# Lead-in of an attention and expert kernel: order of the first loads, row writes and stack loads, and the place of three batches' statistics

## The reference

```
x = x + L0_xattn(layernorm(x), ctx, ctx)   # 16 heads of 16, time bias -0.1 |tq - tk|
x = x + L0_ffn(layernorm(x))               # product-key experts + dense
x = x + L1_xattn(layernorm(x), ctx, ctx)   # relu projections
x = x + L1_ffn(x)                          # 8 experts, top 2
```

## Time and profile before

| what | value |
|---|---|
| time, median of 3 runs | 1219.52 us (1215.89 to 1220.21) |
| the profiled execution: time, span | 1213.62 us, 1211.8 us |
| TensorE, VectorE, ScalarE, GpSimd busy share | 87%, 65%, 53%, 39% |
| chain that ended last, by engine | PE 55%, DVE 24%, ACT 8%, issue 6%, POOL 3%, DMA 3% |
| mean granted clock | 0.928 |

### The profile page before, as it was taken

The page is one execution under the profiler, slowest core; times in us unless marked ns, Lnnn a source line. Parts: engine busy times, 40 slices in busy tenths (PEclk is TensorE's granted clock), DMA queues, the critical chain, the costliest instruction groups (busy, mean ns, idle before and its releaser), DMA issues.

```text
span 1211.8 us, 16920 instructions
## 1 busy us (share of the span) xinstructions
PE 1055.4 (87%) x5478; PEld 658.8 (54%) x5478; DVE 788.4 (65%) x1986; ACT 638.7 (53%) x848; POOL 474.4 (39%) x494
## 2 busy tenths in 40 slices
PE   9499899989776999999999778999999888799991
PEld 5134343434355787787777554433334334588881
DVE  3667677786489777877787334777777955244443
ACT  2146565566528667667677422565545661355550
POOL 1347777686413243343443321212323334222220
PEclk9579999999879999999999986999998998899996
DMA  7946778666999300000002330455453328222226
GB/s 186 249 148 192 228 198 264 174 206 224 255 238 233 78 1 1 1 1 1 1 1 64 103 78 1 148 165 146 117 167 93 102 63 325 66 74 71 72 62 209
DMA packets 75595, 151.71 MB, mean 125 GB/s; under 512 B 8234, under 2 KB 45356, under 8 KB 73974
## 3 DMA queue, kind: packets, MB, share of 16 engines
q1 hardware_dynamic: 62518, 99.46, 31.9%
q0 software_dynamic: 10544, 47.23, 11.2%
q10 hardware_dynamic: 2448, 3.94, 1.2%
HBM read 73.88 MB, written 76.25 MB: 124 GB/s over the span
## 4 chain that ended last, share of the span: by engine, by line
PE 55%; DVE 24%; ACT 8%; issue 6%; POOL 3%; DMA 3%; SPq 1%; ACTq 0%; DVEq 0%; POOLq 0%
PE ps L1296 14%; DVE negmax L1589 9%; PE ps L1194 7%; PE ps L1161 6%; PE ps L1140 4%; PE ps L1175 4%; PE ps L1149 4%; PE ps L1398 3%; PE ps L1375 3%; PE ps L1361 2%; PE ps L1203 1%; PE ps L1516 1%; DVE moe_w L1885 1%; DVE hl L1594 1%; DVE on L1609 1%
## 5 line engine op out<-in xcount | busy, mean ns | idle before, releaser
L1589 DVE TENSOR_REDUCE negmax<-ps 128x1 f32<-128x512 f32 x512 | 320.9, 682 | 68.9 <-PE ps L1161 67.2
L905 ACT ACTIVATE pt<-ps 128x1024 f32<-128x1024 f32 x256 | 256.4, 1026 | 129.9 <-PE ps L1175 129.1
L1161 PE MATMUL ps<-sk,sq 56*128 56x512 f32 x512 | 166.5, 460 | 48.0 <-DVE negmax L1589 24.7
L1194 PE MATMUL ps<-pt,v_aug 128*32 128x512 f32 x1024 | 142.6, 620 | 1.2 <-POOL pt L670 0.8
L1161 PEld LDWEIGHTS ps<-sk,sq 56*128 56x128 f32 x512 | 75.7, 200 | 105.3 <-DVE negmax L1589 76.3
L1175 PE MATMUL ps<-sq,sk 57*128 57x512 f32 x512 | 127.1, 489 | 2.5 <-DVE negmax L1589 1.4
L670 POOL TENSOR_TENSOR pt<-pt,near 128x256 f32<-128x256 f32 x128 | 92.3, 728 | 76.0 <-ACT pt L905 75.7
L1175 PEld LDWEIGHTS ps<-sq,sk 57*128 57x128 f32 x512 | 50.1, 190 | 101.2 <-issue 72.4
L835 POOL DMA_INDIRECT expert_out<-yo,dest x39 | 38.2, 980 | 116.2 <-ACT yo L1080 104.5
L751 POOL TENSOR_TENSOR w_first<-w_first,moe_w 128x1024 f32<-128x1024 f32 x16 | 38.1, 2379 | 105.7 <-DVE pt L1877 105.0
L1361 PE MATMUL ps<-sel,hl 128*128 128x512 f32 x256 | 71.7, 412 | 5.6 <-DVE pt L1877 5.6
(11 more groups left out here) (284 smaller groups left out, 2008.2 us busy)
## 6 DMA issues: line engine op xcount, KB each, us to landing
expert_rows<-zero SPq DMA_DIRECT2D x3, 5586.0 KB, 58.0
expert_weights_split<-wst POOLq DMA_DIRECT2D x8, 2048.0 KB, 9.4
qk_rows<-hl SPq DMA_DIRECT2D x30, 512.0 KB
sq<-qk_rows SPq DMA_DIRECT2D x60, 192.0 KB, 4.6
sk<-qk_rows SPq DMA_DIRECT2D x60, 192.0 KB, 5.1
moe_w<-in_w POOLq DMA_DIRECT2D x16, 512.0 KB, 7.1
wexp<-expert_weights_split POOLq DMA_DIRECT2D x16, 512.0 KB, 4.6
wexp<-expert_weights_split SPq DMA_DIRECT2D x4, 2048.0 KB, 17.1
```

Of the source, the lines that this page charges most:

```text
L905: act.activation(pt[:, 4 * (U % 2) + 2 * half:4 * (U % 2) + 2 * half + 2, :], ps[:, 2 + 2 * half:4 + 2 * half, :], ACT.Exp, scale=(BIAS, S ...
L1161: pe.matmul(ps[:, jbank(job), :], sq[r, pair, t * P:(t + 1) * P], sk[r, pair, :], start=True, stop=True).then_inc(s_job, 1)
L1194: ins = pe.matmul(ps[32 * j:32 * j + 32, OBANK, :], v_aug[:, b % 2, c, HG * g + j, :], pt[:, 4 * (U % 2) + j, :], start=(c == 0), stop=(c ...
L1589: dve.tensor_reduce(negmax[:, n % 2, col:col + 1], src, AX, ALU.max, negate=True).then_inc(s_jd, 1)
```

## The change

It rewrites the order of the lead-in on all engines, and moves the statistics of batches 1 to 3.

- VectorE makes `rowc` first, as soon as its source is in, then batch 0's statistics and norm, then scales the Q weights. Its `prologue()` is gone. The statistics of batches 1, 2 and 3 (`batch_stats`) stand at the ends of steps -4, -3 and -2, the reciprocal at the end of step -1.
- SP issues the constant rows and the rows of K directly behind the constants, then `w_ret` and `keys`, then all eight stacks of K; only when group 0 of both stacks is in does it issue x of batches 1 to 3, the next context and the selector.
- ScalarE issues the rows of Q ahead of emptying V, then all eight stacks of Q. It copies the folded weights out of PSUM, takes the square root of batches 1 to 3 and then `near`'s exponential.
- GpSimd issues six of the weight loads, scales the gate weights, subtracts the low parts of `wret` at steps 4 and 8, and adds `bo` at later steps.
- TensorE runs `keep_busy(4)` behind the folded weights; the gate products stand at the end of step -4. In the first attention K of a batch now stands before its norm's transposes (steps -1 and 0 for batch 1, 11 and 12 for batch 2).

```diff
-STACKS = (None, 10, 12, 12)
-NEXT_CTX = (-LEAD, -9)
+PREPARE_1 = {-17: ("k", 0), -16: ("k", 1), -15: ("xt", 0), -14: ("xt", 1), -13: ("q", 0), -12: ("q", 1), -11: ("v", 0), -10: ("v", 1)}
+PREPARE_2 = {-21: ("k", 0), -20: ("k", 1), -17: ("xt", 0), -16: ("xt", 1), -15: ("q", 0), -14: ("q", 1), -12: ("v", 0), -11: ("v", 1)}
+STACKS = ((None, 10, 11, 11), (None, 10, 12, 12))
+NEXT_CTX = ((2, -9), (-LEAD, -9))
...
+            sp.dma_start(st_rows, a["c_rows"]).then_inc(s_rows_in, 16)
...
             sp.wait_ge(s_rowc, 1)
+            for dst in (sk, sq):
+                for s in range(2):
+                    const_rows(sp, 0, s, dst)
+            for s in range(2):
+                write_rows(0, 0, "k", s)
+            for dst, src in ((st_wq, a["w_ret"].rearrange("(a n) d -> n a d", n=RD)), (st_keys, a["keys"].rearrange("n h p k -> n (h p k)"))):
+                sp.dma_start(dst, src).then_inc(s_wr, 16)
+            sp.wait_ge(s_dk, 64)
+            for g in range(NG):
+                for s in range(2):
+                    stack(0, 0, g, s, sk)
+            sp.wait_ge(s_ld[0], 64)
+            sp.dma_start(x_tok[:, 1], tokens(a["x"][1])).then_inc(s_x[1], 16)
+            load_ctx(0, 1)
+            sp.dma_start(st_sel, a["c_sel"]).then_inc(s_selin, 16)
+            for b in range(2, B):
+                sp.dma_start(x_tok[:, b], tokens(a["x"][b])).then_inc(s_x[b], 16)
...
+            gate_columns()
             norm(0, 1)
+            bias_out()
...
+                    for k in range(KC):
+                        act.wait_ge(s_wret_ps, k + 1)
+                        act.copy(wret[:, 0, k, :], ps[:, 2 + k, :]).then_inc(s_wret, 1)
+                        act.copy(wret_full[:, k, :], ps[:, 2 + k, :]).then_inc(s_wret, 1)
+                    sqrt(1, sd[:, 1:B, :], mv[:, 1:B, :, 1])
+                    act.wait_ge(s_ci, 16 * NCI)
                     act.activation(near[:], st_dist, ACT.Exp, scale=-BIAS).then_inc(s_nr, 1)
...
                 if L == 0:
                     prologue()
+                    keep_busy(4)
+                pe.wait_ge(s_rowin[L], 16 * NROW)
...
+                    if L == 0 and U == -4:
+                        gate_prologue()
...
+                    if L == 0 and U in (-4, -3, -2):
+                        batch_stats(U + 5)
+                        if U == -2:
+                            dve.sem_inc(s_lnv, 1)
+                    if L == 0 and U == -1:
+                        dve.wait_ge(s_lnd, 2)
+                        dve.reciprocal(rstd[:, 1:B, :], sd[:, 1:B, :]).then_inc(s_rstd, 1)
...
+            def batch_stats(b):
+                dve.wait_ge(s_x[b], 16)
+                stats(TT * b, x_tok[:, b], range(TT))
+                moments(TT * b, mv[:, b])
...
+            dve.wait_ge(s_rows_in, 16)
+            dve.tensor_copy(rowc[:], st_rows).then_inc(s_rowc, 1)
             dve.wait_ge(s_x[0], 16)
```

More of the change, by code:

```diff
@@ L611, in _, with gate_columns, wret_low, bias_out @@
                 pool.memset(dst, value).then_inc(s_ms, 1)
+            for dst, src in (
+                (bo_bc[:], a["bo"].rearrange("(a n) -> a n", a=1).broadcast_to([P, D])), (bvc[:], a["bv"]),
+                (gw[:, :, 0:ME], kcut(a["gate"])), (gcol[:, 0:KC], a["gamma"]),
+                (gcol[:, KC:2 * KC], a["beta"]), (wo[:], kcut(a["wo0"])),
+            ):
+                pool.dma_start(dst, src).then_inc(s_w, 16)
+            own = Own(pool, s_pown)
+            def gate_columns():
+                pool.wait_ge(s_w, 16 * NW)
+                for k in range(KC):
+                    own(pool.tensor_scalar(bv_wide[:, k, :], ones[:], bvc[:, k:k + 1], None, ALU.mult))
+                    own(pool.tensor_scalar(gwb[:, k, :], gw[:, k, 0:ME], gcol[:, KC + k:KC + k + 1], None, ALU.mult))
+                own.wait()
+                for k in range(KC):
+                    own(pool.tensor_scalar(gw[:, k, 0:ME], gw[:, k, 0:ME], gcol[:, k:k + 1], None, ALU.mult))
+                own.wait()
+                pool.sem_inc(s_gi, 1)
+            def wret_low(k):
+                pool.wait_ge(s_wret, 2 * k + 2)
+                pool.tensor_tensor(wret[:, 1, k, :], wret_full[:, k, :], wret[:, 0, k, :].bitcast(F32), ALU.subtract).then_inc(s_wrl, 1)
+            def bias_out():
+                pool.wait_ge(s_wret, 2 * KC + 3)
+                pool.tensor_tensor(bo_bc[:], bo_full, bo_bc[:], ALU.add).then_inc(s_bo_bc, 1)
             def norm(L, b, blocks=range(TT)):
[L614 removed]
+                if L:
+                    pool.wait_ge(s_r2, min(b, 2) + 1)
+                else:
+                    pool.wait_ge(s_rstd, 2)
                 if L and b == 1:
```

184 lines of the change are left out of this document (71 added, 113 removed).

## The result

Slower: 1222.93 us (median of 20 runs, 1218.55 to 1230.08) against 1216.78 for the kernel before (20 runs on the same chip, 1211.27 to 1225.78). The ratio is 1.0044, with a 95% interval of 1.0026 to 1.0062, so +5.4 us (3.2 to 7.5), where -4.6 was forecast. The profiled execution took 1221.87 us.

A forecast was written before the change was run, and what follows sets the result against it. A lead-in queue of transfers, then VectorE's row maxima, were taken to bound the start. Terms -9.4 + 5.6 - 1.3 + 0.5 = -4.6 us took 1219.5 to 1214.9 us, range 1208 to 1222.

The forecast's parts named there:

- Term 1: Lead-in: first score at 38.0 in place of 47.4 by both the stacks' and TensorE's ways, -9.4 us; bounds 35 and 43.
- Rival C: Lead-in: K's stacks slow Q's rows, first score at 45.5, +2.9 us, +5.9 with x waited for (1225); chance 0.10.
- Term 2: Steps -4 to -2: three batches' statistics now stand where VectorE is the bound, 3 x 1.86 = +5.6 us, least 3.7.
- rival B: After the first score: VectorE waits up to 3 us for late x, gain eaten, -1.6 us, 1218; chance 0.15.
- What lies beside: Gate products (2.1 us, covered by VectorE's statistics and full banks), ScalarE's copies and GpSimd's norm of batch 1 cost 0.
- Term 3: First exponential: table load moves out of the way, -1.3 us; K's products trading places with transposes 0, bounds -1.5 and +2.
- Term 4: Later steps: changed tables push bytes toward the 2.1 us stack wait near 123.9, +0.5 us, bounds 0 and 2.
- The sum: Whole kernel: the four terms give -4.6 us, from 1219.5 to 1214.9 us.
- the first sign of being wrong: Lead-in: the prediction is wrong if the first score comes before 35 or after 42.
- The third: Sign of being wrong: TensorE's clock comes back before the first exponential, K's products then each saving 1.8 us.
- the engines of the constant rows: Lead-in: transfers from 9 or 8 partitions use only the 9 or 8 lowest-numbered engines; K's rows' 5 us come back whole.

The follow-up runs named there:

- the control: The changed kernel run once more, unaltered: 1221.77 us, ratio 1.0053 to the kernel before.
- wret_early: Changed kernel with the loads of `w_ret` and `keys` issued behind the constants, ahead of the constant rows: 1216.92 us, ratio 1.0006.
- stats_twice: Changed kernel with the statistics of batches 1 to 3 each taken twice at their place: 1232.23 us (6 runs), ratio 1.0132.
- k_stacks_late: `wret_early` with K's stacks issued only when Q's rows are written: 1218.35 us, ratio 1.0024.
- gate_early: Changed kernel with the gate products moved into TensorE's wait ahead of the folded weights: 1221.14 us, ratio 1.003.
- before_new_tables: Kernel before with only the new table and stack steps of batches 2 and 3, and batch 3's norm at steps 21 and 26: 1221.21 us, ratio 1.0035.
- batch3_old: Changed kernel with batch 3 alone given its old rows, stacks and norm steps: 1215.84 us, ratio 1.0001.
- best_x_first: Changed kernel with `wret_early`, `batch3_old`, statistics ahead of the first maximum, early gate products and batch 1's old order: 1212.06 us (7 runs), ratio 0.9937.
- best_stacks_late: `best_x_first` with K's stacks issued only when Q's rows are written: 1210.87 us (12 runs), ratio 0.9958.
- two_fixes: Changed kernel with the edits of `wret_early` and `batch3_old` together: 1211.64 us, ratio 0.9973.
- after_no_busy: Changed kernel without `keep_busy(4)` ahead of the first score: 1221.77 us, ratio 1.0032.
- stats_first: Changed kernel with x of batches 1 to 3 loaded ahead of K's stacks and their statistics taken before the first maximum: 1221.02 us, ratio 1.0034.
- no_steps_work: Changed kernel with statistics ahead of the first maximum and gate products in TensorE's early wait, K's products kept at steps -1 and 0: 1218.51 us, ratio 1.0009.
- after_old_tables: Changed kernel with batches 2 and 3 given their old tables and stack steps, GpSimd's norms moved ahead accordingly: 1223.16 us, ratio 1.0045.

## Why the prediction was wrong, point by point

**Term 1, the first score: -9.4 forecast, -3.5 measured (-2.0 in the control). This is the first step that failed**, at "w_ret is issued near 23.5; I take 5, so 28.5. The product took 3.71 us". It was issued at 22.4, and the last load, `keys`, landed at 31.1 (32.6 in the control): 7.6 and 9.0 us behind its issue, where my own row said 8.6 and I took 5 for no reason that a row gave. And the product ran at the low clock, 7.09 in place of 3.71: TensorE had stood 5 us, the granted clock was at 1.2 GHz from 28.8 to 42.4, and I had put the slow clock only on the loop. Both errors lie on TensorE's own way, 2.6 + 3.4 = 6.0 us; the loop took 5.82, inside its bounds. The other way was off too: group 0 of the stacks was in at 41.7, when SP went on to x, and at 40.2 to 42.0 in the other executions of this lead-in. There Q's rows were written at 32.8 to 33.6, near the 32.3 of the sum, and the stacks took 7 to 9 us in place of 5.7; in the profiled one it was 36.0 and 5.7. So 38 was out of reach by both. `wret_early` shows what the late weights cost: first score 39.8, and 4.9 us of the time. Rival C's size (+2.9 to +5.9) was nearer than the forecast, by luck: its way, K's stacks slowing Q's rows, is not shown, and TensorE's own way was the later one.

**Term 2, the statistics: the length right, the path wrong.** +5.6 was forecast; the pieces are three of 1.8 us, but only the second is on the chain. The third lies beside K's product, as the lower bound of 3.7 had it, and the first beside the gate products, which the sum had put the other way round. Taken away alone the three gave 2.4 us, not 5.6. `stats_twice` shows what statistics cost that nothing covers (6.2 us by step 3 for 5.6 added). x was not waited for in the changed kernel; in `k_stacks_late` it was, 4.35 us, the wait of rival B.

**What lies beside: wrong for the gate products.** I took 0, covered by statistics and full banks. It was the other way: they covered the statistics. They took 3.8 us at the low clock, not 2.1, and VectorE stood 1.86 us behind them; `gate_early` won 2.5 at step 0.

**Term 3, the table load: -1.3 and 0 for K's products.** The square root is at 66.41, the table load at 66.73, and the first exponential at 69.80, 0.7 us behind the first key scores in place of 2.0. So the load is off that place and the 1.3 us are there. Whether the time has them is not shown: the chain of the kernel before passes from the first key scores at 65.03 on through TensorE's work to K's product at 70.34, without the load or the exponential. K's products are the same work, as I said (3.78 and 1.98 us, as in the earlier trace rows), but the first now stands ahead of the first key scores, and it is on the chain, with batch 3's statistics beside it; the 0 should have been 2.4 once the statistics are out of the way. That the spacing of 25.2 lies where 17.4 + 5.6 and VectorE's gap of 1.9 put it (24.9) is in part luck: the chain has the gate products (3.7), one piece of statistics (1.8) and K's product (3.7) in their place.

**Term 4, the later steps: +0.5 forecast, bounds 0 and 2. This is the second step that failed.** I read the one stack wait of the earlier trace rows and looked for its growth. It shrank. What grew was a wait that had not been there: the maximum rows behind both halves of batch 3's K rows and four stacks in SP's queue, 3.6 us. `before_new_tables` measures +4.3 us for the tables, `batch3_old` takes 5.9 back. The profiled traces agree with the sizes: steps 31 to 38 took 35.5 us in place of 30.6. Against the kernel before, the profiled execution is 4.3 us behind at step 0, 2.5 at step 31, 7.4 at step 38 and 8.3 at the end.

**The sum.** The forecast was 10.0 us too low (-4.6 against +5.4). The late weights are 4.9 of it and batch 3's table 5.9 by the medians; with both undone the change gives -3.3 us (-6.1 to -0.6), which holds the forecast. The statistics, the gate products and K's order are then still in it. `best_x_first` and `best_stacks_late`, without them, lie 4.5 and 5.7 us under the kernel before by the medians, where `two_fixes` lies 5.0 under it, so what these three still cost in the time is not shown.

**The signs named.** The first score came after 42, the first sign of being wrong. VectorE waited for no x. The third came too: the clock was back from 42.4 to 49.3, through the first scores, and then low until 69.8, where the first exponential starts. Of what the prediction says on the engines of the constant rows, bears out the count alone (a share of 7.4 engines), not which engines they are. K's rows did start the whole 5 us earlier, Q's stacks only 1.3 to 4.5.

**What the clock gave and took.** A gain at the first score is not a gain at the end. `gate_early` and `stats_first` won 2.5 at step 0 and 1 at step 3. `after_no_busy` won 5 and kept 1. `no_steps_work` was 3.5 us ahead of the control up to step 63 and level some 70 us later, with the same program there; its low stretches had fallen otherwise. The windows of 320 to 400 in `no_steps_work` and then in the control (busy by engine, then clock, DMA share, GB/s):

```profile
320.00:400.00 80.00, 53.57 (x223) 38.70 (x220) 56.82 (x184) 36.42 (x44) 20.12 (x13) 0.83 1.12 253
```
```profile
320.00:400.00 80.00, 53.09 (x244) 37.22 (x242) 59.05 (x189) 39.33 (x47) 22.98 (x16) 0.89 1.11 255
```

Granted 0.83 against 0.89. This is also where the spread of one kernel's executions goes: those of `two_fixes` run from 1206.6 us at a mean granted clock of 0.939 to 1218.6 at 0.924. Why the low stretches fall where they do there is left open; no run was made on it. `after_old_tables`, 5.7 us ahead of the control at step 63 and 5.8 behind at the end, lost its lead in such stretches; why it has more of them is open as well.

## What to carry to other kernels

When a stall at the start is shortened, look for every way into the instruction behind it, and price each from rows of the stretch that it will run in: a product behind a wait of 5 us took 1.9 times its old time. A table that moves large row writes by a step has to be held against the small transfers on the same queue, whose order in the queue is fixed by the program. And when taking work away wins less than adding it costs, something as long lies beside it, and the chain of the profile names it: take both away together before calling either cheap.

## What was unexpected of the hardware

- Transfers of 4 KB moved 8.4 to 8.9 us behind their first issue when 2.3 MB of row writes and stacks had been issued on the same queue in the 8.7 us ahead of it, and 3.9 to 4.9 us behind it where one half of the rows and no stacks were. The Trainium skill (DMA: Bandwidth & Descriptors, Queues, rings and completion order) says that an engine goes round the queues by packets, which rival C used. No run here shows a price for it: K's stacks held back or not, Q's rows were written at 30.6 and 30.5.
- The product of the folded weights took 3.78 us directly behind other work and 7.09 behind a wait of 5 us, with or without the loop behind it. The granted clock is at its lower level in the second case.
- Doubling 5.6 us of statistics on VectorE cost 10.5 us in the median, 6.2 of them by step 3. The rest lies behind step 63, where the program is the same, and goes with a lower granted clock: 397.2 us at 0.94 from there to the second attention where the control has 393.7 at 0.96, and 252.5 at 0.95 in its steps where the control has 249.1 at 0.97. What sets the clock there is not explained.
